# Second layer of a routed expert network: one 512-column and one 256-column matmul per step become three of 256 columns, and the two passes that add the result become one

## The reference, cut to what matters

```python
dispatched = jnp.einsum('sec,sm->ecm', dispatch_mask, x)
h = jax.nn.gelu(jnp.einsum('ecd,edf->ecf', dispatched, w1))
expert_out = jnp.einsum('ecf,efd->ecd', h, w2)
combined = jnp.einsum('sec,ecm->sm', combine_weights, expert_out)
x = x + jnp.tanh(g_ffn[0]) * combined
```

## Time and profile before

| | |
|---|---|
| profiled execution | 122.39 us |
| its span | 120.7 us |
| granted TensorE clock, mean | 0.95 |
| median of three other runs | 123.19 us (121.72 to 125.67) |
| PE busy | 100.0 us, 83% of the span |
| DVE busy | 82.0 us, 68% |
| ACT busy | 73.3 us, 61% |
| POOL busy | 57.6 us, 48% |
| chain that ended last, share of PE | 50% |
| chain, share of L1311 / L1323 / L1325 | 19% / 12% / 6% |

### The profile page before, as it was taken

One profiled execution on the slowest core, in us unless ns is written; L12 is line 12 of the kernel. 1 busy time (PEld: TensorE's weight loads), 2 busy tenths in 40 slices (PEclk: granted clock), 3 DMA queues, 4 the chain that ended last, 5 costly groups with the idle time before them and its releaser, 6 DMA issues.

```text
span 120.7 us, 2208 instructions
## 1 busy us (share of the span) xinstructions
PE 100.0 (83%) x734; PEld 87.7 (73%) x734; DVE 82.0 (68%) x231; ACT 73.3 (61%) x159; POOL 57.6 (48%) x124
## 2 busy tenths in 40 slices
PE   1867387898774699985997999999999999999920
PEld 0356277695652588974986999999998989999810
DVE  1687697979778669754079946768594948667430
ACT  4045589998977768669045516758484939577000
POOL 6348667874997976842776300404050503113042
PEclk9995899999999999995599999999999999999997
DMA  3995999998380204200259799998968310101011
GB/s 107 311 307 168 375 331 369 381 338 281 66 286 0 92 0 160 101 3 0 80 156 369 204 370 421 334 404 286 346 255 293 103 36 0 43 0 49 0 43 43
DMA packets 14090, 22.66 MB, mean 188 GB/s; under 512 B 1287, under 2 KB 11527, under 8 KB 13056
## 3 DMA queue, kind: packets, MB, share of 16 engines
q1 hardware_dynamic: 13312, 20.46, 49.0%
q0 software_dynamic: 768, 2.07, 4.9%
HBM read 20.46 MB, written 2.10 MB: 187 GB/s over the span
## 4 chain that ended last, share of the span: by engine, by line
PE 50%; DVE 12%; POOL 11%; DMA 9%; ACT 5%; SPq 5%; issue 4%; POOLq 1%
PE bk L1311 19%; PE bk L1323 12%; PE bk L1325 6%; DMA gates<-in_g_ffn 6%; DMA gr<-out,gidx 4%; DVE w2p L1058 2%; POOL sc L368 2%; POOL wide_a L362 2%; POOL rsd L398 2%; DVE am L734 2%; PE bk L1231 2%; PE bk L1267 1%; SPq L224 1%; SPq L221 1%; PE bk L1149 1%
## 5 line engine op out<-in xcount | busy, mean ns | idle before, releaser
L467 POOL DMA_INDIRECT out<-xrow,sidx x8 | 10.9, 1361 | 40.1 <-DVE xrow L1078 40.1
L1311 PE MATMUL bk<-rows_w,w_sb 128*128 128x128 f32 x192 | 24.8, 287 | 0.5 <-DVE rows_w L1042 0.5
L1311 PEld LDWEIGHTS bk<-rows_w,w_sb 128*128 128x128 f32 x192 | 23.9, 203 | 1.1 <-DVE rows_w L1042 0.9
L1323 PE MATMUL bk<-w2p,hh 128*128 128x512 f32 x64 | 23.4, 406 | 0.0
L1325 PE MATMUL bk<-w2p,hl 128*128 128x256 f32 x64 | 17.9, 280 | 0.0
L560 ACT ACTIVATE w2p<-w_sb 128x1024 fp32r<-128x1024 f32 x12 | 12.0, 1046 | 8.5 <-PE bk L1325 8.5
L620 ACT ACTIVATE bk<-bk 128x512 f32<-128x512 f32 x16 | 9.3, 581 | 8.9 <-PE bk L1311 8.9
L1058 DVE TENSOR_TENSOR w2p<-w_sb,w2p 128x1024 fp32r<-128x1024 f32 x12 | 14.1, 1218 | 0.3
L1066 DVE TENSOR_TENSOR hl<-bk,hh 128x512 fp32r<-128x512 f32 x16 | 10.9, 685 | 5.0 <-ACT hh L627 5.0
L1323 PEld LDWEIGHTS bk<-w2p,hh 128*128 128x128 f32 x64 | 12.0, 188 | 2.6
L1325 PEld LDWEIGHTS bk<-w2p,hl 128*128 128x128 f32 x64 | 12.1, 189 | 0.0
(11 more groups left out here) (166 smaller groups left out, 228.5 us busy)
## 6 DMA issues: line engine op xcount, KB each, us to landing
w_sb<-in_w SPq DMA_DIRECT2D x12, 1024.0 KB, 6.3
x<-in_x SPq DMA_DIRECT2D x4, 256.0 KB, 3.5
cw<-in_ctx_gu SPq DMA_DIRECT2D x4, 256.0 KB, 4.6
cw<-in_w SPq DMA_DIRECT2D x1, 1024.0 KB, 5.4
out<-x SPq DMA_DIRECT2D x4, 256.0 KB, 2.1
x<-in_w SPq DMA_DIRECT2D x1, 1024.0 KB, 5.6
wide_a<-in_w SPq DMA_DIRECT2D x1, 1024.0 KB, 5.6
wide_b<-in_w SPq DMA_DIRECT2D x1, 1024.0 KB, 7.9
```

Source lines behind the costliest of these rows:

```text
L467: nc.gpsimd.indirect_dma_start(out_rows, bass.IndirectOffsetOnAxis(ap=sidx[:, e:e + 1], axis=0), yo[:, e % 2, :], None, bounds_check=B * T ...
L1311: ins = nc.tensor.matmul(HB[e % 2][:, m, n * C:(n + 1) * C], wv[:, k, f:f + P], xgT[:, e % B, k], start=(k == 0), stop=(k == K - 1))
L1323: nc.tensor.matmul(YB[e % 2], hh[:, e % 2, n], w2p[:, e % 2, n].rearrange("p a d -> p (a d)"), start=(n == 0), stop=False)
```

## The change

In `expert_out` the matmul of 512 columns is cut in two matmuls of 256 columns with the same stationary operand `hh`: one with the high part of `w2`, one with its low part. All three matmuls of a block n now sum into the same 256 columns of the bank. `YB` becomes 256 columns wide. `expert_add` has one instruction, in the form of the former L1076, and it raises `y_ready`. The number of columns that TensorE streams stays 768 for each n; its matmul instructions in this function go from 16 to 24 for each expert, from 128 to 192 in all, and the weight loads likewise. The order of all other work stays.

```diff
--- before.py
+++ after.py
@@ -165,7 +165,7 @@
         GT = bk[3][:, 1, 0:E]
 
         HB = [bk[0], bk[1]]
-        YB = [bk[2][:, 0, :], bk[2][:, 1, :]]
+        YB = [bk[2][:, 0, 0:D], bk[2][:, 1, 0:D]]
         XT = bk[3][:, 0, 0:K * C]
 
         def places(b):
@@ -1073,10 +1073,8 @@
                 dve.wait_ge(rows_here[e], 16)
                 if e >= 2:
                     dve.wait_ge(out_scattered[e % 2], 16 * (e // 2))
-                link(nc.vector.scalar_tensor_tensor(out=yo[:, e % 2], in0=YB[e % 2][:, 0:D], scalar=gt[:, e:e + 1],
-                                                    in1=gr[:, e], op0=ALU.mult, op1=ALU.add))
-                nc.vector.scalar_tensor_tensor(out=yo[:, e % 2], in0=YB[e % 2][:, D:2 * D], scalar=gt[:, e:e + 1],
-                                               in1=yo[:, e % 2], op0=ALU.mult, op1=ALU.add).then_inc(y_ready, 1)
+                nc.vector.scalar_tensor_tensor(out=yo[:, e % 2], in0=YB[e % 2], scalar=gt[:, e:e + 1],
+                                               in1=gr[:, e], op0=ALU.mult, op1=ALU.add).then_inc(y_ready, 1)
 
             expert_in(1)
             split_low(0)
@@ -1320,10 +1318,10 @@
                 for n in range(NF):
                     if n % 4 == 0:
                         pe.wait_ge(hlow_ready, 2 * e + n // 4 + 1)
-                    nc.tensor.matmul(YB[e % 2], hh[:, e % 2, n], w2p[:, e % 2, n].rearrange("p a d -> p (a d)"),
-                                     start=(n == 0), stop=False)
-                    ins = nc.tensor.matmul(YB[e % 2][:, 0:D], hl[:, e % 2, n], w2p[:, e % 2, n, 0],
-                                           start=False, stop=(n == NF - 1))
+                    nc.tensor.matmul(YB[e % 2], hh[:, e % 2, n], w2p[:, e % 2, n, 0], start=(n == 0), stop=False)
+                    nc.tensor.matmul(YB[e % 2], hh[:, e % 2, n], w2p[:, e % 2, n, 1], start=False, stop=False)
+                    ins = nc.tensor.matmul(YB[e % 2], hl[:, e % 2, n], w2p[:, e % 2, n, 0], start=False,
+                                           stop=(n == NF - 1))
                 ins.then_inc(y_used, 1)
 
             fill(3, 0, 6)
```

## The result

The kernel after took 125.63, 126.00, 125.38 and 126.16 us, median 125.81 us. The kernel before got a fourth execution of 125.61 us, so that its median of four is 124.40 us. The ratio is 1.0273 with a 95% interval of 1.0152 to 1.0394: slower, where I had forecast 122.5 us and no measurable change, and outside my range. (Of a kernel's executions only those within about 1.5% of its fastest enter a ratio here, and in the experiments the profiled one does not; medians and means are of all executions, but for one of 171.9 us.) The 1.0273 is thus the mean of all four executions of after, 125.79 us, over the mean of the two shortest of before, 122.46 us; over the mean of all four of before, 124.05 us, it would be 1.014.

A forecast was written before the change was run, and what follows sets the result against it. The prediction took TensorE alone to bound the expert stage; from 122.79 us, +0.26 us for added matmuls and -0.52 us at the end gave 122.5 us, range 120.9 to 124.3 us.

The forecast's parts named there:

- The bound and the streamed columns: Expert stage, 66 to 115.47 us: bound by TensorE alone; 768 columns per n before and after, nothing gained or lost.
- The price of one more matmul: Expert stage on TensorE: one more matmul instruction costs 4 ns per n, 0.26 us in all, bounds -0.6 to +0.6 us.
- Loads and same columns: TensorE in expert_out: 64 more weight loads stay hidden and summing into just-written columns does not stall; both cost 0.
- DVE in the middle: Six experts inside the stage: each loses 0.52 us of DVE time, worth nothing because DVE is not the bound.
- The tail: After the last matmul: one DVE pass remains instead of two, saving 0.52 us; POOL and the last scatter move up.
- The sum over what was changed: Matmul price +0.26 us and end saving -0.52 us together: 0.26 us less than the profiled execution.
- the base: Whole kernel's starting time: 122.79 us, the middle of four known executions, from which 0.26 us was subtracted.
- the lost tail: Rival at the end: the last scatter is held by POOL, so 0.52 us is lost; 123.05 us, 8%.
- The visible load: Rival in the expert stage: one added weight load per n shows, 72 ns each, 4.6 us; 127.1 us, 8%.
- the stall: Rival in the expert stage: summing into the same columns makes matmuls wait, 10.4 us at most; 133 us, 2%.
- the shortest pitch: Rival in the expert stage: 256-column matmuls run at 0.11 us, 22 ns less per n; 120.9 us, 6%.

The follow-up runs named there:

- e3: Kernel before with only the 512-column matmul cut in two, writing left and right 256 columns, both DVE passes kept; median 126.29 us, ratio 1.0107.
- e7: Kernel after with the second and third matmul of each n exchanged (hh, hl, hh); one execution, 125.10 us.
- e1: Kernel before, run again unchanged; 122.61 to 125.75 us, median 125.22 us.
- e2: Kernel after, run again unchanged; median 125.51 us, ratio 1.0145 to the kernel before.
- e5: Kernel before with 29 filler matmuls where TensorE idles between 37 and 66 us; median 122.21 us, ratio 0.9727.
- e6: Kernel after with the same 29 filler matmuls between 37 and 66 us; median 121.96 us, ratio 0.982 to the kernel before.
- e9: Kernel before with only the ten filler matmuls between 37 and 41 us; median 121.31 us, ratio 0.9822.
- e8: Kernel before with 29 fillers, plus three-matmul form and single pass in the last expert only; median 121.05 us, ratio 0.9695 to the kernel before.

## Why the prediction was wrong

**The bound and the streamed columns: right.** TensorE waits for nothing in the stage after, and the 768 columns cost what they did.

**The price of one more matmul: right in kind, too small.** Forecast +4 ns for each n and +0.26 us in all. Measured: of the six experts ahead of the last two, five went from 2.82 to 2.86 or 2.87 us and the first from 2.93 to 2.97 us, and the sixteen last n from 5.56 to 5.76 us, +0.48 us in all. My bounds, -0.6 to +0.6 us, held it. The mis-sized term is the pitch of 256 columns, taken as 0.1175 to 0.119 us from a pair; three in a row run at 0.120 us, in e3 and e7 too. A part of it is a wrong reading: of the eight pieces of L1323 in that stage six are 0.23 and two are 0.24, not five and three. They make 1.86 us, which leaves 0.96/8 = 0.120 us for 256 columns and 0.2325 for 512, hence +7.5 ns, or 0.48 us for 64, as measured; that it agrees so well is luck in part, since the pieces are rounded to 10 ns. At the end, where the pair had been quickest (0.3475 us), the triple takes 0.36 us as elsewhere, so 12.5 ns were lost there instead of my 5.

**Loads and same columns: right in that no gap appears.** Writing to two places instead of one (e3) changes nothing. Whether the 0.48 us are the matmuls' or the loads' is open, as said.

**DVE in the middle: right.** ACT became DVE's new wait (2.6 us over six experts), and nobody waited for DVE.

**The tail: right.** Forecast -0.52 us. From the end of the last matmul to the end of the span: 5.23 and 5.17 us before (first profile and e1), 4.65 and 4.66 after (first profile and e2). By the pieces, free of the rounding of the span, it is 1.60 us down to 1.08, the 0.52 forecast.

**The sum over what was changed: 0.2 us off, by the term above.** Forecast -0.26 us; measured from the first expert_out to the end of the span 50.37 us before and 50.34 after, in the means of three profiles each. That is no change within the rounding; the parts, +0.48 and -0.52 us, add up to -0.04.

**The step that failed is the base.** I wrote: "Of the four times known (121.72, 122.39, 123.19, 125.67) the middle is 122.79 us, which I take as the kernel's time." The kernel's median over 65 executions is 125.15 us. The profile that I read was the one without a fall of the clock between 40 and 51 us, and the allowance of 1.2 us for scatter above the lost tail was too small: the base lay 2.4 us below the median, and executions lie anywhere in 121.7 to 129.4 us. The slices of the earlier trace rows showed two falls, and I passed over them, because they lay before the changed part. With 125.15 - 0.26 = 124.9 us as the forecast, 125.81 us would have been near. As far as the larger sample shows, the measured ratio of 1.0273 is for the most part the draw of the six executions that it rests on: 65 and 22 of them differ by +0.5 us with 0.8 us either way, and the kernel before against itself once gave 1.0138. What the change itself does to the clock, up to about 1.3 us, stays open.

**The rivals.** The visible load (127.1 us) came nearest to the time, but not for its reason: 64 x 72 ns would show as 4.6 us in the stage, and the stage grew by 0.48 us of pitch. The lost tail, the stall and the shortest pitch did not happen. The Trainium skill, "TensorE: Matmul & The Clock Gate", section "HAM oscillation — how this bites in real kernels", describes a matmul kernel in which TensorE waits for a DMA after every short burst of matmuls; in each such wait its clock falls, and the next burst starts at the lower rate. The waits described there are longer than the gaps here. The trace agrees in kind and shows the same with short gaps. TensorE's timeline of the kernel after has these rows:

```profile
38.70 0.66 PE L1209 MATMUL bk<-ident,wide_b 128*128 128x128 f32 x4 [1.52 <-ACT wide_b L527]
...
41.10 0.19 PE L1246 MATMUL bk<-onehot,upper_own 128*128 128x8 bf16 x1 [1.05 <-DVE onehot L847]
```

It idles for 1.52 and 1.05 us, and the clock is down from about 41 to 48 us; with those gaps filled it is not (e5, e6, e9). The profiled execution of before had the same two gaps (1.52 and 1.06 us) and no fall, so the gaps make it possible and not certain. Had I weighed that page against the idle stretches ahead of the stage, I would have had a reason for a wider range.

## What to carry to other kernels

Split the profiled span at the first changed instruction: what lies before it and still differs between the two profiles is not the change. Here 3.3 us lay before it and -0.1 us after it, of the 3.2 us between the two spans. When short gaps on TensorE precede a long matmul stage, look at the granted clock there before pricing anything small, and expect single executions to differ by microseconds. Ten filler matmuls in such gaps were worth more (ratio 0.9822, about 2 us) than the 0.52 us that the change could have given at best. A pass removed behind a bound engine pays only where it is on the path, the last expert, so by the profiles (49.90 us in e8 against 50.41 in e5) the new form belongs there alone.

## What the runs showed of the hardware that was not expected

- Ten matmuls of 512 columns, put into two gaps of together 2.6 us, made the kernel faster although they are added work: the mean is 121.03 us in six executions, against 125.91 us in the eleven of the kernel before beside it, 4.9 us less with 1.5 us either way. By the ratio, 0.9822, which rests on the two shortest executions of the kernel before, it is about 2.2 us.
- 768 columns in F32R take 0.3475 us at the end and 0.3525 us in the middle of the stage as a pair of 512 and 256, and 0.36 us in both places as three matmuls of 256, whether or not the stationary operand repeats.
- One execution of the kernel before took 171.9 us at a mean granted clock of 0.559. It is left out of all figures above.
